# A fused attention, norm and gate layer: the last two steps spread their roots in fp32, half an output product moves ahead, and a search changes place with a tanh

## The chip, the cores and the metric

The kernel runs on one core of one Trainium2 chip. Its time is the device time of one execution in microseconds (us), and the metric is the median over runs. Before the change it is 129.13 us (three runs, 128.83 to 129.57).

## The reference

The input x is [4, 512, 256] in fp32. Cut to what matters, with 16 heads of 16 columns:

```
xn = layernorm(x)
q, k, v = silu(xn @ Wq), silu(xn @ Wk), silu(xn @ Wv)
o  = linear attention with a decay for each head, causal
o  = o * sigmoid((xn @ Wg1) @ Wg2)
og = o * rsqrt(mean(o * o over a head's 16 columns) + 1e-5) * norm_w
s  = og @ Wo
f  = fp8 rounding of (xn * scale), times fp8 rounding of W2, descaled
out = x + s * silu(f)
```

So each output element needs a root for its token and head. A root is computed once for each (token, head) and has to be spread over the 16 columns of the head.

## The kernel before

The work is cut into `STEPS` = 8 steps. A step takes 128 tokens of each of two sequences (`S` = 2, so 256 tokens); steps 0, 2, 4, 6 walk along sequences 0 and 1, steps 1, 3, 5, 7 along sequences 2 and 3. Data lie transposed, channels on the 128 partitions in two halves (`KH` = 2) and tokens along the free side, so that a step's tile of o is 128 x 512. Five engines work side by side, and the order of each engine's instructions is written out by hand: a prologue, a loop over steps 1 to 6, and an epilogue for step 7. Semaphores tie them together; an engine executes its own instructions in order, so a wait holds up all that stands behind it. Step n's scores and outputs overlap with step n+1's projections and with step n-1's norm.

The path of one step through the norm and the output:

- TensorE (PE): `scores(n)`; VectorE (DVE): four `mask(n, r)`, which multiply the scores by the decay mask; PE: `from_state(n)` and `from_chunk(n, half, s)`, which make o; DVE: `gate_o(n)`, which makes og; ScalarE (ACT): `square_o(n)`; PE: `head_sums(n)`, which adds the squares of a head.
- The root: in steps 6 and 7 ACT's `square_root(n)` and DVE's `root_last(n)` (a reciprocal and three small operations on 128 x 64), which leave the root in `rs_full`, in PSUM.
- The spread: `root_pair_last(n)` on DVE splits the root in a rounded part (`rs_hi`, in the fp32r format) and a remainder (`rs_pair`), and multiplies them by `own_block` into `rs_spread` (128 x 256, fp32r). Then PE's `spread_rs(n)` multiplies that with `head_spread`, two matmuls, and adds `rs_in_psum` (`s_rsps`).
- `head_norm(n)` on DVE multiplies og by the spread root into `on`; in step 7 `head_norm_last(s)` does so for each sequence.
- `project_o(n, s)` on PE multiplies `on` by the output weights: in steps 0 to 5 with six fp32r matmuls for each sequence, in steps 6 and 7 with two fp32 matmuls. `product(n)` on DVE multiplies by the silu of f, and `add_x(n)` on POOL (GpSimd) adds x; in step 7 `product_last(s)` and `add_x_last(s)` do both on DVE. SyncE (SP) issues the stores in the order of the steps.

In the epilogue, PE runs `from_chunk(7)`, `spread_rs(6)`, `project_o(5, 1)` (the second half of the output of step 5), `head_sums(7)`, `project_o(6)`, `spread_rs(7)`, three `keep_warm` matmuls on the identity, whose result nobody uses, and `project_o(7)`. DVE runs `root_last(6)`, `root_pair_last(6)`, `gate_o(7)`, `head_norm(6)`, `root_last(7)`, `root_pair_last(7)`, `product(5)`, `head_norm_last`, `product(6)`, and then the last products and sums.

In the prologue, the fp8 rounding of step 1 goes from POOL's `round_y(1)` (it writes `e4_q`) to ACT's `find_over(1)` (values that overflow fp8, into `b_s`), to DVE's `put_nan(1)` (writes `xqT`), to PE's `ffn(1)`. `gate(1)` on ACT is the tanh of step 1's gate. Its result is first wanted by `scores(1)` and `gate_o(1)`. ACT runs `copy_kT(1)`, `gate(1)`, `find_over(1)`, `high_xT(2)`.

`low_xT(2)` and `gate_o(0)` on DVE and `silu_ffn(1)` and `scale_y(2)` on ACT stand behind these in their engines' orders.

Of the kernel before, what the change touches and what calls it, by code (L numbers as in the profile page):

```python
# [5 lines left out]
F32 = mybir.dt.float32  # L6
# [7 lines left out]
P = 128  # L14
# [3 lines left out]
def layer_kernel(nc, x, log_decay, Wq, Wk, Wv, Wo, Wg1, Wg2, norm_w, W2, scale, scale1, out):  # L18
# [27 lines left out]
    with ExitStack() as ctx:  # L46
        def sb(name, shape, dt=F32):
            return ctx.enter_context(nc.sbuf_tensor(name, shape, dt))

        def sem(name):  # L50
            return ctx.enter_context(nc.semaphore(name))
# [19 lines left out]
        root_var = sb("root_var", [P, 2, C])  # L71
        root_sqrt = sb("root_sqrt", [P, 2, C])
        root_inv = sb("root_inv", [P, 2, C])
        wg2_stack = sb("wg2_stack", [P, D], F32R)
        w2_f32 = sb("w2_f32", [P, KH, D])
        w2_y = sb("w2_y", [P, KH, D])
# [110 lines left out]
        ps_u_last = b_x[:, W // 2:W].rearrange("p (k s e) -> p k s e", k=KH, s=S)  # L187
        ps_o_last = b_kv[:].rearrange("p (c z) -> p c z", c=2)[:, :, 0:256]
        ps_out_last2 = b_o[:, 0:512].rearrange("p (s n) -> p s n", s=S)
        ps_rs_last2 = b_o[:, 512:1024].rearrange("p (k t) -> p k t", k=KH)  # L190
        ps_sum_last = b_s[:, 0:C]
        ps_prod_last = [b_kv[:, 0:D], b_kv[:, 512:512 + D]]
# [78 lines left out]
        s_rs = sem("og_rs_steps")  # L271
        s_sqrt = sem("last_square_roots_ready")
        s_lastrs = sem("last_rs_steps")
        s_spread = sem("rs_spread_ready")
        s_rsps = sem("rs_in_psum")
        s_on = sem("on_ready")
# [11 lines left out]
        def need(eng, s, v):  # L288
            if v > 0:
                eng.wait_ge(s, v)  # L290
# [234 lines left out]
        def _(act):  # L525
# [56 lines left out]
            def gate(n):  # L582
                act.wait_ge(s_gateps, n + 1)
                need(act, s_og, n - 1)
                dst = gate_tanh[:, n % 2].rearrange("p c (z t) -> p z c t", z=KH * S)
                src = ps_gate.rearrange("p k (s c t) -> p (k s) c t", s=S, c=2)
                a.activation(dst, src, ACT.Tanh, scale=0.5).then_inc(s_gate, 1)
# [8 lines left out]
            def copy_kT(n):  # L596
                act.wait_ge(s_kTps, n + 1)
                need(act, s_score, n - 1)
                a.activation(kT[:, n % 2], ps_kT, ACT.Copy).then_inc(s_kT, 1)
# [74 lines left out]
            act.wait_ge(s_w2q, 4)  # L674
            a.activation(w2_over[:], w2_q[:], ACT.Copy, scale=E4_OVER).then_inc(s_w2q, 1)
            copy_kT(1)
            gate(1)
            find_over(1)
            high_xT(2)
            act.wait_ge(s_dvec, 4)  # L680
            silu_ffn(1)
# [40 lines left out]
        def _(dve):  # L722
# [137 lines left out]
                v.scalar_tensor_tensor(out=rs_full, in0=rs_err, scalar=-3.0 / ROOT_SCALE, in1=root_inv[:, u],  # L860
                                       op0=ALU.add, op1=ALU.mult).then_inc(s_lastrs, 1)

            def root_pair_last(n):

                k = 4 * (n - (STEPS - 2))
                j = RS_STEPS * (STEPS - 2) + 2 * (n - (STEPS - 2))
                dve.wait_ge(s_lastrs, k + 4)
                v.tensor_copy(rs_hi[:], rs_full).then_inc(s_rs, 1)
                dve.wait_ge(s_rs, j + 1)
                v.scalar_tensor_tensor(out=rs_pair, in0=rs_hi[:].bitcast(F32), scalar=head_parity[:, 1:2], in1=rs_full,  # L870
                                       op0=ALU.mult, op1=ALU.subtract).then_inc(s_rs, 1)
                dve.wait_ge(s_rs, j + 2)
                need(dve, s_rsps, n)
                v.scalar_tensor_tensor(out=rs_spread[:], in0=rs_pair.unsqueeze(1).broadcast_to([P, 4, C]), scalar=-1.0,
                                       in1=own_block[:].unsqueeze(2).broadcast_to([P, 4, C]), op0=ALU.mult, op1=ALU.mult).then_inc(s_spread, 1)

            def head_norm_last(s):
                n = STEPS - 1
                dve.wait_ge(s_rsps, n + 1)
                dve.wait_ge(s_og, n + 1)  # L880
                dve.wait_ge(s_outps, S * (n - 1))
                v.tensor_tensor(on[:, n % 2].rearrange("p k (s c t) -> p s k c t", s=S, c=2)[:, s],
                                og[:, n % 2].rearrange("p c (k s t) -> p s k c t", k=KH, s=S)[:, s],
                                ps_rs.rearrange("p k (s c t) -> p s k c t", s=S, c=2)[:, s], ALU.mult).then_inc(s_onlast, 1)

            def product_last(s):
                n = STEPS - 1
# [111 lines left out]
            gate_o(0)  # L999
            dve.wait_ge(s_pec, 1)  # L1000
            v.tensor_scalar(head_spread[:], ps_spread, -0.75, None, ALU.mult).then_inc(s_dvec, 1)
            exponent(2)
            magic(2)

# [28 lines left out]
            for r in (2, 3, 0, 1):  # L1033
                mask(n, r)
            root_last(n - 1)
            root_pair_last(n - 1)
            gate_o(n)
            head_norm(n - 1)
            root_last(n)
            root_pair_last(n)  # L1040

            product(n - 2)
            for s in range(S):
                head_norm_last(s)
            product(n - 1)
# [5 lines left out]
        def _(pe):  # L1051
# [219 lines left out]
            def spread_rs(n):  # L1271
# [4 lines left out]
                                  start=(half == 0), stop=True, skip_group_check=True)  # L1276
                mm.then_inc(s_rsps, 1)

            def project_o(n, s):
                if n == STEPS - 1:  # L1280
                    pe.wait_ge(s_onlast, s + 1)
                elif s == 0:
                    pe.wait_ge(s_on, n + 1)
                    if known(n + 2):

                        pe.wait_ge(s_mid, mids(n + 1))
                        pe.wait_ge(s_end, ends(n + 1))
                    elif n == STEPS - 2:

                        pe.wait_ge(s_probs, 4 * STEPS)  # L1290
                dst = ps_out[:, s] if n < STEPS - 2 else ps_out_last2[:, s] if n < STEPS - 1 else ps_last[s]
                if n < STEPS - 2:
                    tok = slice(s * P, s * P + P)
                    pe.wait_ge(s_onhi, n + 1)
                    pe.wait_ge(s_woready, 4)
                    for kk in range(KH):
                        t.matmul(dst, on_hi[:, kk, tok], wo_hi[:, kk], start=(kk == 0 and s == 0), stop=False, skip_group_check=True)
                    pe.wait_ge(s_wolo, 1)
                    for kk in range(KH):
                        t.matmul(dst, on_hi[:, kk, tok], wo_lo[:, kk], start=False, stop=False, skip_group_check=True)  # L1300
                    pe.wait_ge(s_onlo, n + 1)
                    for kk in range(KH):
                        mm = t.matmul(dst, on_lo[:, kk, tok], wo_hi[:, kk], start=False, stop=(kk == KH - 1), skip_group_check=True)
                    mm.then_inc(s_outps, 1)
                    return
                for kk in range(KH):
                    mm = t.matmul(dst, on[:, n % 2, kk, s * P:s * P + P], wo_scaled[:, kk], start=(kk == 0 and (s == 0 or n == STEPS - 1)),  # L1307
                                  stop=(kk == KH - 1), skip_group_check=True)
                mm.then_inc(s_outps, 1)
# [89 lines left out]
            scores(n)  # L1399
            head_sums(n - 1)  # L1400
            from_state(n)
            from_chunk(n, 0, 0)
            from_chunk(n, 0, 1)
            from_chunk(n, 1, 0)
            from_chunk(n, 1, 1)
            spread_rs(n - 1)
            project_o(n - 2, 1)
            head_sums(n)
            project_o(n - 1, 0)
            project_o(n - 1, 1)  # L1410
            spread_rs(n)

            keep_warm(3, b_k)
            for s in range(S):
                project_o(n, s)

# [26 lines left out]
```

## Time and profile before

| | |
|---|---|
| median of three runs | 129.13 us (128.83 to 129.57) |
| the profiled execution | 128.68 us |
| its span | 126.9 us |
| PE busy | 114.7 us (90%) |
| DVE busy | 101.7 us (80%) |
| ACT busy | 81.4 us (64%) |
| POOL busy | 80.8 us (64%) |
| mean granted TensorE clock | 0.994 of full speed |

The profiled execution is 1.78 us longer than its span: that part lies around the instructions that the profile records. PE's busy share is an average: matmuls are pipelined and their ends are modelled. In the stretch of the loop it is near 100%, and in the epilogue (from 110.7 us) it falls to six or seven tenths, with DVE at eight or nine.

### The profile page before, as it was taken

To read this page: it belongs to the slowest core of one execution; us is meant where nothing else is said; L and a number is where in the kernel's file an instruction comes from. 1 tells how busy PE (TensorE), PEld (TensorE's weight loads), DVE (VectorE), ACT (ScalarE), POOL (GpSimd) and SP (SyncE) were. 2 spreads that over 40 slices of the span, in tenths; PEclk is the share of its full clock that TensorE was granted. 3 is DMA by queue.
4 is the path that set the end of the run, shared out by engine and by line. 5 is a ranking of instruction groups with operands and counts; after the bars stand their busy time and mean duration, and the time that the engine had idled before them with its cause. 6 is when DMAs were issued, how large, how long until landed. Compare 5 with 4: busy or idle time off the path is not lost.

```text
span 126.9 us, 6394 instructions
## 1 busy us (share of the span) xinstructions
PE 114.7 (90%) x2688; PEld 99.3 (78%) x2688; DVE 101.7 (80%) x271; ACT 81.4 (64%) x156; POOL 80.8 (64%) x119
## 2 busy tenths in 40 slices
PE   3979989988999999999999999999999999867680
PEld 3979889758978898879978898889788987556560
DVE  1899999989895899869994999498939891497781
ACT  7689989969967656684677378558673664811100
POOL 6716599899839683968677884968384839100070
PEclk9999999999999999999999999999999999999997
DMA  2769800020000400033003300150006040000015
GB/s 84 235 175 339 273 3 3 5 45 6 5 0 10 83 0 5 5 62 108 3 5 65 111 0 5 41 132 5 0 20 150 5 126 5 5 5 5 0 67 181
DMA packets 11067, 7.57 MB, mean 60 GB/s; under 512 B 4832, under 2 KB 11040, under 8 KB 11040
## 3 DMA queue, kind: packets, MB, share of 16 engines
q1 hardware_dynamic: 11040, 7.17, 20.2%
q8 instruction: 21, 0.34, 1.1%
q14 instruction: 6, 0.05, 0.1%
HBM read 3.50 MB, written 2.10 MB: 44 GB/s over the span
## 4 chain that ended last, share of the span: by engine, by line
POOL 31%; issue 29%; DVE 20%; ACT 9%; PE 6%; DMA 2%; POOLq 0%; DVEq 0%
POOL e_q L408 5%; POOL e_sum L403 5%; POOL y L441 5%; POOL kd L419 4%; DVE probs L764 4%; POOL rstd L396 3%; POOL own_mid L423 2%; POOL qd L413 2%; DMA x_sb<-in_L_attn_x_dram 2%; POOL on_lo L446 1%; PE b_s L1307 1%; DVE bn L729 1%; POOL own_end L423 1%; DVE og L797 1%; DVE xqT L754 1%
## 5 line engine op out<-in xcount | busy, mean ns | idle before, releaser
L1092 PE MATMUL b_kv<-w_hi,xT_hi 128*128 128x256 f32 x64 | 16.8, 284 | 0.0
L1093 PE MATMUL b_kv<-w_lo,xT_hi 128*128 128x256 f32 x64 | 16.5, 281 | 0.0
L441 POOL TENSOR_TENSOR y<-sg,x_sb 128x512 f32<-128x512 f32 x7 | 9.0, 1286 | 10.4 <-DVE sg L902 10.3
L446 POOL TENSOR_TENSOR on_lo<-on,on_hi 128x512 fp32r<-128x512 f32 x6 | 7.7, 1278 | 12.3 <-ACT on_hi L620 12.3
L403 POOL TENSOR_TENSOR e_sum<-e_y,e_magic 128x512 f32<-128x512 f32 x8 | 10.3, 1285 | 7.2 <-DVE e_magic L748 7.2
L797 DVE SCALAR_TENSOR_TENSOR og<-gate_tanh,b_o 128x512 f32<-128x512 f32 x7 | 4.8, 687 | 11.8 <-PE b_o L1243 11.8
L1095 PE MATMUL b_kv<-w_hi,xT_lo 128*128 128x256 f32 x64 | 12.7, 280 | 0.0
L1243 PE MATMUL b_o<-probs,v_par 64*32 64x64 f32 x896 | 12.6, 222 | 0.0
L413 POOL TENSOR_TENSOR qd<-q_silu,q_decay 128x512 f32<-128x512 f32 x8 | 10.3, 1293 | 3.3 <-ACT q_silu L550 3.3
L1092 PEld LDWEIGHTS b_kv<-w_hi,xT_hi 128*128 128x128 f32 x64 | 12.0, 188 | 0.2 <-issue 0.2
L1093 PEld LDWEIGHTS b_kv<-w_lo,xT_hi 128*128 128x128 f32 x64 | 12.1, 188 | 0.0
L1243 PEld LDWEIGHTS b_o<-probs,v_par 64*32 64x32 f32 x896 | 8.4, 106 | 4.2 <-issue 2.5
L764 DVE TENSOR_TENSOR probs<-b_o,decay_mask 128x512 f32<-128x512 f32 x16 | 10.3, 686 | 1.1 <-PE b_o L1174 1.1
L408 POOL TENSOR_TENSOR e_q<-e_sum,e_magic 128x512 bf16<-128x512 f32 x8 | 10.8, 1345 | 0.5
L550 ACT ACTIVATE q_silu<-b_q 128x512 f32<-128x512 f32 x8 | 4.8, 598 | 9.7 <-PE b_q L1084 9.7
L1174 PE MATMUL b_s<-q_par,kT 32*64 32x128 f32 x256 | 9.3, 276 | 1.0 <-DVE og L797 0.7
L764 DVE TENSOR_TENSOR probs<-b_s,decay_mask 128x512 f32<-128x512 f32 x16 | 10.2, 681 | 0.0
L555 ACT ACTIVATE q_par<-b_q,head_parity 128x512 f32<-128x512 f32 x16 | 10.1, 684 | 0.0
L1095 PEld LDWEIGHTS b_kv<-w_hi,xT_lo 128*128 128x128 f32 x64 | 9.8, 188 | 0.0
L1174 PE MATMUL b_o<-q_par,kT 32*64 32x128 f32 x256 | 9.5, 278 | 0.0
L1174 PEld LDWEIGHTS b_s<-q_par,kT 32*64 32x64 f32 x256 | 7.6, 131 | 2.4 <-issue 2.2
L604 ACT ACTIVATE og_sq<-og 128x512 f32<-128x512 f32 x8 | 5.0, 631 | 6.8 <-DVE og L797 6.8
(205 smaller groups left out, 366.6 us busy)
## 6 DMA issues: line engine op xcount, KB each, us to landing
out_dram<-y SPq DMA_DIRECT2D x7, 256.0 KB, 2.5
x_sb<-in_L_attn_x_dram SPq DMA_DIRECT2D x4, 384.0 KB, 5.4
own_cross<-own_end SPq DMA_DIRECT2D x12, 64.0 KB, 2.0
qd_cross<-qd SPq DMA_DIRECT2D x12, 64.0 KB, 2.4
x_sb<-in_L_attn_x_dram SPq DMA_DIRECT2D x2, 256.0 KB, 3.5
w_f<-in_L_attn_Wq_dram SPq DMA_DIRECT2D x1, 256.0 KB, 3.8
w_f<-in_L_attn_Wk_dram SPq DMA_DIRECT2D x1, 256.0 KB, 4.0
w_f<-in_L_attn_Wv_dram SPq DMA_DIRECT2D x1, 256.0 KB, 4.5
```

What stands on the lines that cost most here:

```text
L403: g.tensor_tensor(e4_sum[:], e4_y[:, n % 2], e4_magic[:, n % 2], ALU.add).then_inc(s_e4sum, 1)
L408: g.tensor_tensor(e4_q[:], e4_sum[:], e4_magic[:, n % 2], ALU.subtract).then_inc(s_e4q, 1)
L413: g.tensor_tensor(qd[:, n % 2].rearrange("p k (s t) -> p k s t", s=S), q_silu[:].rearrange("p k (s t) -> p k s t", s=S), q_decay[:].unsque ...
L441: g.tensor_tensor(y[:, n % 2], sg[:, n % 2].rearrange("p (s d) -> p s d", s=S), x_sb[:, x_tiles(n), :], ALU.add).then_inc(s_y, 1)
L446: g.tensor_tensor(on_lo[:], on[:, n % 2], on_hi[:].bitcast(F32), ALU.subtract).then_inc(s_onlo, 1)
L555: a.activation(q_par[:, n % 2, par], ps_q, ACT.Silu, scale=head_parity[:, par:par + 1]).then_inc(s_qpar, 1)
L764: v.tensor_tensor(probs[:, r], ps_score[r].rearrange("p (s z) -> p s z", s=S), decay_mask[:, r].unsqueeze(1).broadcast_to([P, S, 4 * C]), ...
L1092: t.matmul(dst[:, s], xT_hi[:, u, kk, tok], w_hi[:, w, kk], start=(s == 0 and kk == 0), stop=False, skip_group_check=True)
L1093: t.matmul(dst[:, s], xT_hi[:, u, kk, tok], w_lo[:, w, kk], start=False, stop=False, skip_group_check=True)
L1095: mm = t.matmul(dst[:, s], xT_lo[:, u, kk, tok], w_hi[:, w, kk], start=False, stop=(kk == KH - 1), skip_group_check=True)
L1174: mm = t.matmul(ps_score[r][c * C:c * C + C, cols], kT[rows, u, half, tok], q_par[rows, u, :, half, tok], start=True, stop=True, skip_grou ...
L1243: mm = t.matmul(dst[32 * r:32 * r + 32, c, z:z + C], v_par[rows, u, blk:blk + 2 * E], probs[rows, r, s, i:i + C], start=(half == 0 and s = ...
```

## The change

It has three parts.

1. In steps 6 and 7 the roots are spread in fp32. `root_blocks(n)` replaces `root_pair_last(n)`: one DVE operation multiplies `rs_full` by `own_first` into `rs_blocks` (128 x 256, fp32). `own_first`, 128 x 4, is a new constant, made once in the prologue by one DVE operation. `spread_blocks` replaces `spread_rs`: the same two matmuls, both operands now fp32. In step 7 it is called for each sequence, with half the columns each, into two PSUM areas, and `head_norm_last(s)` waits for its own one. The `keep_warm` calls are two instead of three, and stand ahead of the spread.
2. `project_o(5, 1)` on PE moves from behind `spread_rs(6)` to ahead of `from_chunk(7)`; `product(5)` on DVE moves from behind the roots of step 7 to between `gate_o(7)` and `head_norm(6)`.
3. On ACT, `find_over(1)` comes ahead of `gate(1)`.

```diff
+        own_first = sb("own_first", [P, 4])
+        rs_blocks = sb("rs_blocks", [P, 2, 4, C])
...
+        ps_rs_last = [b_x[:, 0:T], b_o[:, 512:512 + T]]
...
             copy_kT(1)
+            find_over(1)
             gate(1)
-            find_over(1)
             high_xT(2)
...
-            def root_pair_last(n):
-
-                k = 4 * (n - (STEPS - 2))
-                j = RS_STEPS * (STEPS - 2) + 2 * (n - (STEPS - 2))
-                dve.wait_ge(s_lastrs, k + 4)
-                v.tensor_copy(rs_hi[:], rs_full).then_inc(s_rs, 1)
-                dve.wait_ge(s_rs, j + 1)
-                v.scalar_tensor_tensor(out=rs_pair, in0=rs_hi[:].bitcast(F32), scalar=head_parity[:, 1:2], in1=rs_full,
-                                       op0=ALU.mult, op1=ALU.subtract).then_inc(s_rs, 1)
-                dve.wait_ge(s_rs, j + 2)
-                need(dve, s_rsps, n)
-                v.scalar_tensor_tensor(out=rs_spread[:], in0=rs_pair.unsqueeze(1).broadcast_to([P, 4, C]), scalar=-1.0,
-                                       in1=own_block[:].unsqueeze(2).broadcast_to([P, 4, C]), op0=ALU.mult, op1=ALU.mult).then_inc(s_spread, 1)
+            def root_blocks(n):
+
+                u = n % 2
+                dve.wait_ge(s_lastrs, 4 * (n - (STEPS - 2)) + 4)
+                dve.wait_ge(s_ownfirst, 1)
+                v.tensor_tensor(rs_blocks[:, u], rs_full.unsqueeze(1).broadcast_to([P, 4, C]),
+                                own_first[:].unsqueeze(2).broadcast_to([P, 4, C]), ALU.mult).then_inc(s_spread, 1)
 
             def head_norm_last(s):
                 n = STEPS - 1
-                dve.wait_ge(s_rsps, n + 1)
+                dve.wait_ge(s_rsps, n + s + 1)
...
-                                ps_rs.rearrange("p k (s c t) -> p s k c t", s=S, c=2)[:, s], ALU.mult).then_inc(s_onlast, 1)
+                                ps_rs_last[s].rearrange("p (k c t) -> p k c t", k=KH, c=2), ALU.mult).then_inc(s_onlast, 1)
...
             v.tensor_scalar(head_spread[:], ps_spread, -0.75, None, ALU.mult).then_inc(s_dvec, 1)
+            dve.wait_ge(s_hpar, 2)
+            v.tensor_scalar(own_first[:], own_block[:], head_parity[:, 0:1], None, ALU.mult).then_inc(s_ownfirst, 1)
             exponent(2)
             magic(2)
...
             root_last(n - 1)
-            root_pair_last(n - 1)
+            root_blocks(n - 1)
             gate_o(n)
+            product(n - 2)
             head_norm(n - 1)
             root_last(n)
-            root_pair_last(n)
-
-            product(n - 2)
+            root_blocks(n)
             for s in range(S):
                 head_norm_last(s)
             product(n - 1)
...
+            def spread_blocks(n, dst, blocks):
+
+                pe.wait_ge(s_spread, n + 1)
+                for half in range(KH):
+                    mm = t.matmul(dst[:, half], head_spread[:, half].bitcast(F32), rs_blocks[:, n % 2, blocks].rearrange("p j t -> p (j t)"),
                                   start=(half == 0), stop=True, skip_group_check=True)
                 mm.then_inc(s_rsps, 1)
...
             from_state(n)
+
+            project_o(n - 2, 1)
             from_chunk(n, 0, 0)
             from_chunk(n, 0, 1)
             from_chunk(n, 1, 0)
             from_chunk(n, 1, 1)
-            spread_rs(n - 1)
-            project_o(n - 2, 1)
+            spread_blocks(n - 1, ps_rs_last2, slice(0, 4))
             head_sums(n)
             project_o(n - 1, 0)
             project_o(n - 1, 1)
-            spread_rs(n)
-
-            keep_warm(3, b_k)
+
+            keep_warm(2, b_k)
+            for s in range(S):
+                if s == 1:
+                    pe.wait_ge(s_on, n)
+                spread_blocks(n, ps_rs_last[s].rearrange("p (k t) -> p k t", k=KH), slice(2 * s, 2 * s + 2))
             for s in range(S):
                 project_o(n, s)
```

## Rows read from the trace of the kernel before

**Rows 1.** The page's chain that ended last, shares of the span by engine.

```profile
POOL 31%; issue 29%; DVE 20%; ACT 9%; PE 6%; DMA 2%; POOLq 0%; DVEq 0%
```

**Rows 2.** Stretches: start:end, length, busy time per engine, granted clock, DMA share, GB/s.

```profile
33.00:45.00 12.00, 11.91 (x314) 10.06 (x313) 9.91 (x25) 8.23 (x17) 8.92 (x12) 1.00 0.12 25
...
119.30:120.28 0.98, 0.00 (x0) 0.00 (x1) 0.91 (x4) 0.00 (x0) 0.00 (x0) 1.00 0.00 0
```

**Rows 3.** Timeline of ACT, prologue: start, length, engine, line, operation, out<-in, shapes, [idle before].

```profile
24.86 0.59 ACT L587 ACTIVATE gate_tanh<-b_s 128x512 f32<-128x512 f32 x1
25.35 0.59 ACT L562 ACTIVATE b_s<-e_q 128x512 f32<-128x512 bf16 x1
25.87 0.59 ACT L540 ACTIVATE xT_hi<-b_x 128x512 fp32r<-128x512 f32 x1
```

**Rows 4.** Timeline of POOL, prologue.

```profile
23.22 1.73 POOL L408 TENSOR_TENSOR e_q<-e_sum,e_magic 128x512 bf16<-128x512 f32 x1
...
31.30 1.29 POOL L408 TENSOR_TENSOR e_q<-e_sum,e_magic 128x512 bf16<-128x512 f32 x1
```

**Rows 5.** Timeline of DVE, prologue.

```profile
23.01 0.80 DVE L989 SCALAR_TENSOR_TENSOR w_q<-w_f,w_m 128x512 bf16<-128x512 f32 x1
...
24.63 0.87 DVE L995 SCALAR_TENSOR_TENSOR w_fp<-w_over,w_q 128x512 bf16<-128x512 bf16 x1
25.98 0.69 DVE L754 SCALAR_TENSOR_TENSOR xqT<-b_s,e_q 128x512 bf16<-128x512 f32 x1 [0.48 <-ACT b_s L562]
...
30.11 1.29 DVE L764 TENSOR_TENSOR probs<-b_o,decay_mask 128x512 f32<-128x512 f32 x2 [0.25 <-PE b_o L1174]
```

**Rows 6.** Timeline of PE, prologue.

```profile
26.77 0.60 PE L1145 MATMUL b_s<-w_fp,xqT 128*128 128x256 bf16 x4 [0.52 <-issue]
```

**Rows 7.** Timeline of DVE, epilogue.

```profile
114.60 0.22 DVE L868 CAST rs_hi<-b_x 128x64 fp32r<-128x64 f32 x1
...
115.18 0.42 DVE L874 SCALAR_TENSOR_TENSOR rs_spread<-b_x,own_block 128x256 fp32r<-128x256 f32 x1
115.52 0.68 DVE L797 SCALAR_TENSOR_TENSOR og<-gate_tanh,b_kv 128x512 f32<-128x512 f32 x1
116.20 0.69 DVE L845 TENSOR_TENSOR on<-og,b_o 128x512 f32<-128x512 f32 x1
117.76 0.55 DVE L853 RECIPROCAL root_inv<-root_sqrt 128x64 f32<-128x64 f32 x1 [0.87 <-ACT root_sqrt L614]
...
120.14 0.68 DVE L902 TENSOR_TENSOR sg<-b_q,ffn_silu 128x512 f32<-128x512 f32 x1
120.82 0.75 DVE L882 TENSOR_TENSOR on<-og,b_x 128x256 f32<-128x256 f32 x2
121.49 0.68 DVE L902 TENSOR_TENSOR sg<-b_o,ffn_silu 128x512 f32<-128x512 f32 x1
...
123.79 0.42 DVE L896 TENSOR_TENSOR y<-b_kv,x_sb 128x256 f32<-128x256 f32 x1
```

**Rows 8.** Timeline of PE, epilogue.

```profile
113.28 1.68 PE L1243 MATMUL b_kv<-probs,v_par 64*32 64x64 f32 x128 [1.25 <-DVE probs L764]
115.66 0.50 PE L1275 MATMUL b_o<-rs_spread,head_spread 128*128 128x256 f32 x2 [0.70 <-DVE rs_spread L874]
...
120.62 0.83 PE L1313 MATMUL b_kv<-ident 128*128 128x128 f32 x6
121.29 1.99 PE L1307 MATMUL b_s<-wo_scaled,on 128*128 128x256 f32 x8
```

**Rows 9.** Timeline of ACT, epilogue.

```profile
116.23 0.63 ACT L604 ACTIVATE og_sq<-og 128x512 f32<-128x512 f32 x1 [4.23 <-DVE og L797]
```

**Rows 10.** Timeline of POOL and of SP's queue, the last stores.

```profile
120.90 2.61 POOL L441 TENSOR_TENSOR y<-sg,x_sb 128x512 f32<-128x512 f32 x2 [10.32 <-DVE sg L902]
...
123.54 0.37 SPq L361 DMA_DIRECT2D out_dram<-y  x1
...
123.96 0.96 SPq L378 DMA_DIRECT2D out_dram<-y  x2
```

More of the change, by code:

```diff
@@ L273, in layer_kernel @@
         s_lastrs = sem("last_rs_steps")
+        s_ownfirst = sem("own_first_ready")
         s_spread = sem("rs_spread_ready")
@@ L1277, in spread_rs @@
                 mm.then_inc(s_rsps, 1)
+            def spread_blocks(n, dst, blocks):
+                pe.wait_ge(s_spread, n + 1)
+                for half in range(KH):
+                    mm = t.matmul(dst[:, half], head_spread[:, half].bitcast(F32), rs_blocks[:, n % 2, blocks].rearrange("p j t -> p (j t)"),
+                                  start=(half == 0), stop=True, skip_group_check=True)
+                mm.then_inc(s_rsps, 1)
             def project_o(n, s):
```

## The prediction

> **What bounds the kernel now.** I read the page's chain of waits first, then the busy time by stretch, then the timelines of each engine around the two places that the diff touches. The chain names POOL with 31% and "issue" with 29% [rows 1], but in the loop PE is busy 11.91 of 12.00 us, DVE 9.91, POOL 8.92, ACT 8.23 [rows 2]: TensorE has hardly a gap there, and nothing in the diff is in that stretch. Two stretches are left. In the prologue PE sits idle 0.52 us ahead of the fp8 product of step 1 [rows 6], which waits for DVE's xqT; that one waited 0.48 us for ACT's overflow search [rows 5], which ran at 25.35, right behind the tanh [rows 3]. In the epilogue one chain runs through all engines: masks, o, og (115.52), its square (116.23), head sums, root (117.76), spread (120.28), on (120.82), two fp32 output products (121.29 to 123.28), last sum (to 124.21), stores [rows 7 to 10]. PE is idle for 1.25 us ahead of o [rows 8], and for all of 119.30 to 120.28 while DVE finishes the root; the clock stays at 1.00 there, 2.4 GHz [rows 2].
>
> Times below are on the clock of the old trace. The sum is made against the profiled execution's 128.68 us, which is 0.45 under the median of 129.13; the predicted time is put back on the median's level.
>
> **Part 3, the search first.** The search needs POOL's e_q, which ends at 23.22 + 1.73 = 24.95 [rows 4]. ACT is free for it at 24.86, where the tanh now starts [rows 3]. So it starts at about 25.02 in place of 25.35, and xqT at 25.65 in place of 25.98: 0.33 us. Bounds: ACT's slot allows 0.49 and DVE is busy until 24.63 + 0.87 = 25.50 [rows 5], so at most 0.46; POOL's ends are rough, and the search ran at 25.35 without a wait, so at least 0. I take 0.33, by the row's end. The tanh moves from 24.86 to about 25.51, first wanted by the scores of step 1, just ahead of the masks at 30.11 [rows 5]: covered. The copy xT_hi moves from 25.87 to 26.02 and ends at 26.61; its reader on DVE stands behind xqT (ends at 26.34) and four statistics operations: covered, and late by no more than 0.15 if they took no time. PE's product has been waiting 0.52 [rows 6], so it follows by the full 0.33, and behind it ACT's silu, DVE's og of step 0 and the scores of step 1, from which PE runs without a gap. POOL's work up to e_q of step 2 (ends 32.59 [rows 4]) doesn't move, but its reader on ACT, the search of step 2, stands in the loop behind seven operations of that step. I find nothing after that which stays at an absolute time, so the 0.33 reaches the end.
>
> The new constant own_first is one DVE instruction on 4 columns; the nearest row, 64 columns, takes 0.22 [rows 7]. It goes ahead of the exponents of step 2, and DVE has 0.25 of idle time before the masks that follow [rows 5]: cost 0, at most 0.2 if that cover were gone.
>
> **Part 2, the moved half.** project_o(5,1) is six fp32r matmuls of the shape of the spread's two, which take 0.50 [rows 8]: at most 1.5 us, and about 0.9 if they follow one another at 0.12, as the two do. It falls in the 1.25 us in which PE waits for the masks (112.03 to 113.28) [rows 8]; its inputs are those of project_o(5,0), which ran in step 6. Cost 0, at most 0.25 by the upper figure. What it frees: PE has nothing between the spread of step 6 and the head sums.
>
> product(5), 0.68 us with 0.61 from its start to the next one's, leaves the place where it covered PE's last spread (120.14) [rows 7] and stands ahead of head_norm(6). That is weighed below.
>
> **Part 1, step 6.** Removed on DVE: a cast and the pair, 114.60 to 115.18, 0.58 us; the block product is the same 128 x 256 at 0.42 [rows 7]. Blocks: 114.60 to 115.02. og then waits for PE's o, which ends at 113.28 + 1.68 = 114.96 [rows 8]: start 115.05 in place of 115.52, so only 0.47 of the 0.58 is kept. Its square ends at 116.39 (was 116.86 [rows 9]).
>
> The fp32 spread has no row of its own; two fp32 matmuls of the same shape are in L1307: 8 records, two for each matmul, in 1.99 us with the last 0.38 long, so 0.23 a record [rows 8]. Four records: 3 x 0.23 + 0.38 = 1.07 us in place of 0.50, 115.08 to 116.15. Bounds: 0.50 (no dearer than fp32r) and 1.76 (each record double). I take 1.07, since shape and type are the same. The head sums, queued behind it on PE, are due at 116.45: 0.30 of slack. DVE: product(5) from 115.66, head_norm(6) from 116.27 (the spread is there at 116.20), on(6) at 116.96, 0.07 later than now (116.89 [rows 7]). Then project_o(6) from 117.02, and PE is free at 117.02 + 8 x 0.23 = 118.86. Two keep_warm calls are 4 of the old 6 records, 0.11 each [rows 8]: 119.31.
>
> **Step 7.** The root follows og: reciprocal at 117.29 in place of 117.76. Less the 0.58, blocks end at 119.17 in place of 120.22. PE would take them at 119.23, but is free at 119.31. Each sequence's spread is 4 records of 0.11, the last 0.28 long: first ready at 119.31 + 0.33 + 0.28 = 119.92, second at 120.37. on of sequence 0: 119.97 to 120.39 (was 120.82 to 121.24). project_o(7) starts at 120.45 in place of 121.29 and ends at 122.44: 0.84 gained, and the last y ends at 123.37 in place of 124.21 [rows 7].
>
> The end is set by the queue beside it, though. The second on half starts at 120.42, product(6) at 120.76 in place of 121.49 [rows 7]; POOL adds x (its second sum, to 123.51 [rows 10]), SP issues the store of step 6 at 123.54 and the two last ones behind it from 123.96, back to back [rows 10]. The last one left at about 124.45, 0.24 after its data. All of this moves by product(6)'s 0.73, and store 5 is long gone by then. The epilogue gives 0.73.
>
> Sum: 0.33 + 0.73 = 1.06. 128.68 - 1.06 = 127.62 us; at the median's level 128.07.
>
> **Rivals.** (a) The search gives nothing: e_q arrives at 25.3 and not at 24.95. For it: POOL's spans are rough. Against: a row says 24.95, and nothing else holds the search. Gain 0.73: 128.40.
>
> (b) POOL's addition for step 5, which now runs beside the last root, holds up the DVE. product(5) ends at 116.34, so POOL works from 116.40 to 117.68 (half of 2.61 [rows 10]), where today it is idle; the reciprocal is due at 117.29. For it: POOL's e_q took 1.73 beside DVE's w_q, which reads two tensors in SBUF (23.01 to 23.81), and 1.29 at 31.30 [rows 4, 5], so the two engines do hold each other up. Against: the reciprocal reads one tensor, and the operation behind it, which reads two, is due at 117.95. If the reciprocal waited for POOL, it is 0.39 late, the blocks come at 119.56 and PE starts on them at 119.62, not 119.31: 0.31 lost, gain 0.75: 128.38. The Trainium skill ("SBUF", section on the two separate sides) says that VectorE and GpSimd have one pair of ports in common, taken exclusively for a whole instruction by whichever comes first, on VectorE's side only in a two-port mode or with two SBUF inputs; the two e_q rows agree in kind (0.44 longer). By that rule the reciprocal goes free and only a later start of POOL, by 0.27 or more, would cost anything.
>
> (c) Slower: the fp32 spread costs more than the output product's records say, since its weights are fresh each time and it stands in PE's queue ahead of the head sums, of project_o(6) and of the last step. With records twice as far apart, spread 6 ends at 116.84, on(6) at 117.58, PE is free at 119.93, and the second half's spread is ready at 121.75. product(6) starts at 122.14, 0.65 later than now, and with POOL and SP behind it the end as well; less the 0.33 of the search, 0.32 slower: 129.45. It decides from 1.8 times the record's spacing. Against: L1307 changes its weights with every matmul too and shows 0.23.
>
> **How the numbers follow.** Forecast 50%; (a) 22%; (b) 10%; (c) 8%; 10% for more (the search's 0.46, or the second half's spread less late and the last store bound by its data's 0.84: 1.3, 127.83). About 0.5%, 0.65 us, is what a measurement here can tell from no change. Faster by more than that: 0.45 of the forecast's 0.50, half of (a) and of (b) (0.16), since they lie just over the line, and 0.08 of the last: 0.69. Slower: half of (c) and a little, 0.05. Same: 0.26. The range goes from the larger gain with a fast median to half of what lies between (a) and (c): 127.5 to 129.0.
>
> **What would show it.** Right: xqT of step 1 some 0.3 us earlier and PE's gap ahead of it near 0.2; the six matmuls ahead of o without moving o; a spread of 4 records in about 1.07 us in step 6 and 0.6 for a half in step 7; product(6) 0.73 earlier relative to the masks of step 7, and the last stores back to back behind the store of step 6. Wrong: on(6) more than 0.2 late behind a longer spread; a reciprocal that starts when POOL's y ends; masks of step 7 at the old time.

## The result and the profile after

The changed kernel takes 128.55 us (median of 20 runs) where the kernel before took 128.84 in 20 runs beside it. The ratio is 0.9951 with an interval of 0.9929 to 0.9974: 0.63 us faster, between 0.34 and 0.92. The forecast was 1.06 (a ratio of 0.9918), so the direction was right and the size was not: 1.06 lies outside the interval. The ratio is that of the mean times without the slower runs; four of the changed kernel's that it leaves out took only 129.53 to 129.75, and with every run below 140 us counted on both sides it would be 0.9968, some 0.4 us. The profiled execution took 128.26 us with a span of 126.4 (before 128.68 and 126.9), at a granted clock of 1.000.

First the page after: busy time of the engines, the chain that ended last, and the queue of the instruction transfers (number, MB, share).

```profile
PE 116.2 (92%) x2694; PEld 100.5 (79%) x2694; DVE 100.8 (80%) x268; ACT 81.4 (64%) x156; POOL 80.9 (64%) x119
...
POOL 31%; issue 29%; DVE 17%; PE 8%; ACT 8%; DMA 2%; POOLq 0%; DVEq 0%
...
q8 instruction: 21, 0.34, 1.1%
```

DVE's share of the chain fell from 20% to 17% [rows 1] and PE's rose from 6% to 8%. The third line is one that I did not look at before I predicted; it turns out to matter.

The prologue on ACT, the answer to [rows 3]:

```profile
25.06 0.60 ACT L566 ACTIVATE b_s<-e_q 128x512 f32<-128x512 bf16 x1
25.60 0.58 ACT L591 ACTIVATE gate_tanh<-b_s 128x512 f32<-128x512 f32 x1
```

On DVE, the answer to [rows 5] in its first, third and fourth line (the second is the new constant), and then the epilogue, the answer to [rows 7]:

```profile
25.70 0.69 DVE L758 SCALAR_TENSOR_TENSOR xqT<-b_s,e_q 128x512 bf16<-128x512 f32 x1
...
28.70 0.22 DVE L1001 TENSOR_SCALAR own_first<-own_block,head_parity 128x4 f32<-128x4 f32 x1
...
29.83 1.29 DVE L768 TENSOR_TENSOR probs<-b_o,decay_mask 128x512 f32<-128x512 f32 x2
...
110.37 1.29 DVE L768 TENSOR_TENSOR probs<-b_o,decay_mask 128x512 f32<-128x512 f32 x2 [0.86 <-PE b_o L1173]
...
114.22 0.42 DVE L872 TENSOR_TENSOR rs_blocks<-b_x,own_first 128x256 f32<-128x256 f32 x1
...
115.25 0.69 DVE L801 SCALAR_TENSOR_TENSOR og<-gate_tanh,b_kv 128x512 f32<-128x512 f32 x1 [0.61 <-PE b_kv L1242]
115.86 0.69 DVE L900 TENSOR_TENSOR sg<-b_q,ffn_silu 128x512 f32<-128x512 f32 x1
116.46 0.68 DVE L849 TENSOR_TENSOR on<-og,b_o 128x512 f32<-128x512 f32 x1
...
117.50 0.55 DVE L857 RECIPROCAL root_inv<-root_sqrt 128x64 f32<-128x64 f32 x1 [0.37 <-ACT root_sqrt L618]
...
118.96 0.42 DVE L872 TENSOR_TENSOR rs_blocks<-b_x,own_first 128x256 f32<-128x256 f32 x1
...
120.97 0.69 DVE L900 TENSOR_TENSOR sg<-b_o,ffn_silu 128x512 f32<-128x512 f32 x1
...
123.17 0.42 DVE L894 TENSOR_TENSOR y<-b_kv,x_sb 128x256 f32<-128x256 f32 x1
```

PE after, first the product of step 1 in the prologue, the answer to [rows 6], then the epilogue, the answer to [rows 8]:

```profile
26.49 0.60 PE L1144 MATMUL b_s<-w_fp,xqT 128*128 128x256 bf16 x4 [0.16 <-issue]
...
111.58 0.50 PE L1304 MATMUL b_q<-wo_hi,on_hi 128*128 128x256 f32 x2
...
112.90 1.00 PE L1242 MATMUL b_kv<-probs,v_par 64*32 64x64 f32 x77 [0.35 <-DVE probs L768]
114.47 0.74 PE L1242 MATMUL b_kv<-probs,v_par 64*32 64x64 f32 x51 [0.56 <-issue]
115.14 1.13 PE L1282 MATMUL b_o<-rs_blocks,head_spread 128*128 128x256 f32 x4
...
119.02 0.61 PE L1320 MATMUL b_kv<-ident 128*128 128x128 f32 x4
119.47 0.69 PE L1282 MATMUL b_x<-rs_blocks,head_spread 128*128 128x128 f32 x4
119.99 0.61 PE L1282 MATMUL b_o<-rs_blocks,head_spread 128*128 128x128 f32 x4
120.67 1.99 PE L1314 MATMUL b_s<-wo_scaled,on 128*128 128x256 f32 x8
```

Last, the stores on POOL and on SP's queue, the answer to [rows 10]:

```profile
116.62 1.27 POOL L445 TENSOR_TENSOR y<-sg,x_sb 128x512 f32<-128x512 f32 x1 [6.43 <-DVE sg L900]
121.74 1.27 POOL L445 TENSOR_TENSOR y<-sg,x_sb 128x512 f32<-128x512 f32 x1 [3.85 <-DVE sg L900]
```

```profile
123.03 0.37 SPq L365 DMA_DIRECT2D out_dram<-y  x1
123.45 0.96 SPq L382 DMA_DIRECT2D out_dram<-y  x2
```

Reading these against before: the first mask of step 1 is 0.28 earlier (29.83, was 30.11), the first mask of step 7 is 0.38 earlier (110.37, was 110.75), the last y starts another 0.24 earlier (123.17, was 123.79). The last stores are issued 0.51 earlier (123.45, was 123.96), so 0.13 beyond the masks. The forecast had 0.33 for both masks, and beyond them 0.84 for the last y and 0.73 for the stores. The search's part is there in this profile; more than two thirds of the epilogue's gain are missing. And one pair of rows is strange: the 128 equal matmuls of step 7's from_chunk fall into 77 and 51, with 0.56 us between them that "issue" ends, which is to say that no semaphore does. The forecast had them in one piece of 1.68.

In what follows, a **stop** is the time between the starts of two neighbouring weight loads on PE where the next block of instructions is suspected; in from_chunk the loads are normally 0.01 apart. Its place is the number of the second load, counted from PE's first, which is number 0. In after the stop is 0.83 us in front of load 2595.

### The profile page after: what moved, and what is told of

Read it like the earlier page. It is cut to its first block, busy times and chain, and to the rows that moved or that the text cites. A ratio compares the mean times of both kernels' runs of the same rounds, so it can differ in the third digit from the quotient of the medians.

```text
span 126.4 us, 6404 instructions
## 1 busy us (share of the span) xinstructions
PE 116.2 (92%) x2694; PEld 100.5 (79%) x2694; DVE 100.8 (80%) x268; ACT 81.4 (64%) x156; POOL 80.9 (64%) x119
## 4 chain that ended last, share of the span: by engine, by line
POOL 31%; issue 29%; DVE 17%; PE 8%; ACT 8%; DMA 2%; POOLq 0%; DVEq 0%
POOL e_q L412 5%; POOL y L445 5%; POOL e_sum L407 5%; POOL kd L423 4%; DVE probs L768 4%; POOL rstd L400 3%; POOL own_mid L427 2%; POOL qd L417 2%; DMA x_sb<-in_L_attn_x_dram 2%; PE b_s L1314 2%; PE b_o L1314 2%; POOL on_lo L450 2%; PE b_kv L1242 1%; DVE bn L733 1%; POOL own_end L427 1%
## 5 line engine op out<-in xcount | busy, mean ns | idle before, releaser
L1242 PE MATMUL b_o<-probs,v_par 64*32 64x64 f32 x896 | 12.6, 222 | 0.0
```

What stands on the lines that cost most here:

```text
L1242: mm = t.matmul(dst[32 * r:32 * r + 32, c, z:z + C], v_par[rows, u, blk:blk + 2 * E], probs[rows, r, s, i:i + C], start=(half == 0 and s = ...
```

## The experiments

The theory after the first comparison: the stop is PE waiting for the next block of its own instructions. The rival: it belongs to the place, the inputs or the neighbours of that code. A second question was what each part of the change is worth alone. Each kernel was timed in turns with the kernel before on the same chip. Medians of different jobs differ by some tenths, so ratios are compared.

**Search alone, and epilogue alone.** In the first, the kernel before with

```diff
-            gate(1)
             find_over(1)
+            gate(1)
```

and in the second the changed kernel with these two put back.

> Only the third part of the change, on the kernel before: find_over(1) ahead of gate(1) on ACT. It separates the prologue's share. Theory: xqT of step 1 is some 0.3 us earlier, PE passes it on undiminished, and the masks of step 7 start 0.3 us earlier (110.75 before, about 110.4): ratio about 0.9975. Rival: TensorE's stream later gives it back, for example by waiting for its own instructions: ratio 1.000, masks of step 7 at the old time.

> The changed kernel with gate(1) back ahead of find_over(1): parts one and two alone. In the profile of the changed kernel PE stops for 0.56 us in the middle of from_chunk(7), with no semaphore behind it, which leaves the epilogue 0.24 us of gain where 0.73 were forecast. Theory (the stop is a wait for the next block of PE's instruction stream, whose arrival is tied to an absolute cadence): with the masks 0.3 us later the stop is shorter by that, about 0.25 us, and the epilogue alone gains about 0.5 us: ratio 0.996. Rival (the stop is something of the place, such as the moved project_o or the order of the tiles, and keeps its length): gain 0.24, ratio 0.998.

Measured: 0.9983 [0.9950, 1.0017] for the search alone, 0.9940 [0.9907, 0.9973] for the epilogue alone. PE's from_chunk of step 7, first with the search alone, then with the epilogue alone:

```profile
113.65 1.05 PE L1243 MATMUL b_kv<-probs,v_par 64*32 64x64 f32 x83 [1.11 <-DVE probs L764]
115.53 0.69 PE L1243 MATMUL b_kv<-probs,v_par 64*32 64x64 f32 x45 [0.83 <-issue]
```

```profile
113.89 1.85 PE L1242 MATMUL b_kv<-probs,v_par 64*32 64x64 f32 x128 [0.35 <-DVE probs L768]
```

The search alone has the old code at this point and the stop is there too, 1.08 us; the epilogue alone has the new code and a short one of 0.37, inside the 1.85. So the stop does not belong to the new epilogue. Both lengths are off my expectations: I had the masks of step 7 at about 110.4 in the search alone, and they came at 111.11, later than before's 110.75; and in the epilogue alone I had expected some 0.25 of idle time and a ratio of 0.996. An arrival at a fixed time doesn't fit either, since the masks of the two are only 0.24 apart (111.11 and 111.35) and the stops 0.71. From first mask of step 7 to last y the search alone took 13.44 (before 13.04), the epilogue alone 12.34. The time of the search alone settles nothing: 0.33 us is 0.26%, and the interval is 0.34% to either side.

**Moving the instructions.** If the stop sits at an instruction number, more instructions in the prologue shift the code under it. In these four kernels small matmuls, whose results nobody reads, take the place of part of keep_warm, which fills idle time there; only their number differs (20 here for 72 more instructions; 40, 15 and 34 for 152, 52 and 128).

```diff
-            keep_warm(10, ps_score[1])
+            keep_warm(8, ps_score[1])
+            pad_queue(20)
...
+            def pad_queue(count):
+                for i in range(count):
+                    rows = slice(C * (i % 2), C * (i % 2) + C)
+                    r = (i // 2) % 4
+                    t.matmul(ps_score[i % 2][32 * r:32 * r + 32, 0:C], ident[rows, 0:32], ident[rows, 0:C],
+                             start=True, stop=True, skip_group_check=True)
```

> The changed kernel with 72 more PE instructions in the prologue: keep_warm(10) becomes keep_warm(8) and 20 small matmuls on the identity whose result nobody uses (each is four instructions, two weight loads and two matmul passes), in PE's idle time before x arrives. Nothing else moves. Theory (the stop in from_chunk(7) is at a block boundary of PE's instruction stream, counted in instructions): the stop moves from behind weight load 77 of 128 to about weight load 41, and is longer by the 0.4 us that PE gets there earlier, about 0.9 us, if the block arrives at the same time. Rival (it belongs to the place): still behind about load 77, same length.

> As the kernel with 72 more instructions, but 40 small matmuls, 152 more PE instructions in the prologue. Theory (block boundary): the boundary moves 76 weight loads earlier, to about the first of from_chunk(7), where PE waits for the masks anyway, so that most of the stop is hidden and the o of step 7 is ready up to 0.5 us earlier than in the changed kernel: ratio to before about 0.992, if no other dense stretch is hit. Rival (it belongs to the place): stop behind load 77 and the changed kernel's time, ratio 0.995.

> 52 more PE instructions in the prologue (keep_warm(8) and 15 small matmuls in place of keep_warm(10)). Theory (block boundary): the block boundaries at weight loads 2470 and 2595 now fall on the scores of step 7 and on about load 51 of 128 of from_chunk(7); between the two PE has about 4 us instead of 3 in the changed kernel, so there is no stop, or one under 0.3 us, and the last y comes 12.1 to 12.3 us after the first mask of step 7 (12.80 in the changed kernel): ratio 0.991 to 0.993 if the boundaries in the loop cost no more than before. Rival (a stop of the place): 0.995 and a stop behind load 77 of from_chunk(7).

> 128 more PE instructions in the prologue (keep_warm(8) and 34 small matmuls). Theory (block boundary): the boundary at 2595 falls on about load 13 of 128 of from_chunk(7), 4 us behind the one before, no stop there; but the next one, at about 2723, now falls into PE's last 48 weight loads, which come 3 us later: a stop there of up to 1 us, in front of the fp32 spread or what follows. Ratio 0.992 to 1.002. Rival (a stop of the place): 0.995 and a stop behind load 77.

Measured ratios: 72 more 0.9941 [0.9914, 0.9968], 152 more 1.0034 [0.9989, 1.0078], 52 more 0.9999 [0.9964, 1.0033], 128 more 0.9944 [0.9913, 0.9974]. PE with 72 more instructions: the first row of the step-1 scores, then from_chunk of step 7.

```profile
30.57 0.33 PE L1173 MATMUL b_s<-q_par,kT 32*64 32x128 f32 x2 [1.08 <-issue]
...
115.41 1.48 PE L1242 MATMUL b_kv<-probs,v_par 64*32 64x64 f32 x128 [0.62 <-DVE probs L768]
```

The second row is the one to see: 128 matmuls in one piece of 1.48 us, shorter than the 1.68 of before and of the forecast. My expectation of a stop near the 41st load was wrong: there was none. Earlier ones, the first of them in the row above it and another of 0.75 in front of load 1846, had made step 7 late (from_chunk starts 2.51 us after it does in after), and I take it that the block had arrived by then: the queue's transfer for it began at 113.41, 2.00 us ahead of from_chunk, where in after it began at 111.92, 0.98 us ahead. With no stop, the last y starts 12.13 us after the first mask.

With 152 more, from_chunk is in one piece too, but the stop has gone to the next boundary, load 2723, and that load is in the fp32 spread of step 6:

```profile
113.59 1.48 PE L1242 MATMUL b_kv<-probs,v_par 64*32 64x64 f32 x128 [0.35 <-DVE probs L768]
115.37 0.48 PE L1282 MATMUL b_o<-rs_blocks,head_spread 128*128 128x256 f32 x1 [0.30 <-DVE rs_blocks L872]
117.38 0.92 PE L1282 MATMUL b_o<-rs_blocks,head_spread 128*128 128x256 f32 x3 [1.52 <-issue]
```

One record, 1.5 us of nothing, three records, all of the same kind, on inputs that were all there for the first: no theory of inputs makes such a row. After it the clock fell as well (last section), and mask to y became 15.61. That is not every execution: in six of the twelve the mean clock was 0.984 or 0.985 as in this one, and in the others 0.993 to 0.999. With 128 more the same load 2723 is in the head sums, which come in two groups of eight:

```profile
116.90 0.32 PE L1266 MATMUL b_s<-og_sq,head_sum 128*32 128x64 f32 x8
117.68 0.32 PE L1266 MATMUL b_s<-og_sq,head_sum 128*32 128x64 f32 x8 [0.47 <-issue]
```

With 52 more the stop is 0.19 in front of 2595, again inside from_chunk, and mask to y is 12.16, as with 72. Yet its time is that of the kernel before, where I had expected 0.991 to 0.993: its profile has stops of 0.54 in front of 470, ahead of the first masks of step 1, and of 0.92 in front of 1470 (0.48 in before). In this profile, what the epilogue won, stops elsewhere took.

**The unchanged kernel again, and fewer instructions.** In the second, keep_warm(10) gives way to three longer matmuls, 28 instructions fewer.

```diff
-            keep_warm(10, ps_score[1])
+            for _ in range(3):
+                t.matmul(ps_score[1][:, 0:3 * P].rearrange("p (a b) -> p a b", a=3), ident[:],
+                         ident[:].unsqueeze(1).broadcast_to([P, 3, P]), start=True, stop=True)
```

> The changed kernel once more, as the reference for the three layouts beside it and for a second profile. Theory (PE stops where it reaches a block of its instruction stream that has not arrived yet): if there is a stop in from_chunk(7) at all it is again in front of weight load 2595 counted from PE's first, with another length than 0.7 us, since the arrival varies; other stops only at 470, 1470, 1845 or the like. Rival (a stop of the place): the same length at the same load. Ratio to before 0.995.

> 28 fewer PE instructions in the prologue: the ten warm-up matmuls of 128 columns become three of 384 columns. Theory (block boundary): the boundary at 2595 falls on about load 91 of from_chunk(7), so a stop in from_chunk(7) is behind about load 91, up to 0.7 us long; ratio 0.993 to 0.997. Rival (a stop of the place): behind load 77.

Measured: 0.9957 [0.9918, 0.9995] again (the medians of all runs, 129.38 and 129.45, hardly differ), 1.0020 [0.9982, 1.0058] with 28 fewer. PE of the two:

```profile
113.39 1.00 PE L1242 MATMUL b_kv<-probs,v_par 64*32 64x64 f32 x77 [0.36 <-DVE probs L768]
114.69 0.74 PE L1242 MATMUL b_kv<-probs,v_par 64*32 64x64 f32 x51 [0.30 <-issue]
```

```profile
113.94 1.12 PE L1242 MATMUL b_kv<-probs,v_par 64*32 64x64 f32 x91 [0.36 <-DVE probs L768]
115.50 0.63 PE L1242 MATMUL b_kv<-probs,v_par 64*32 64x64 f32 x37 [0.44 <-issue]
```

The cut is at the same 77 as in after. Fourteen loads fewer ahead of it put it at 77 + 14 = 91, to the load. The place is fixed by count. The stop's length is not: 0.57 where after's profile had 0.83. Why 28 fewer are no faster than before isn't settled; its profile has two stops in the loop, 0.88 in front of 1094 and 0.48 in front of 968.

**Parts of the epilogue.** First the fp32 spread with both moves and the search put back; then the kernel before with the two moves only; then the changed kernel with product(5) behind the roots again.

```diff
             gate_o(n)
+            product(n - 2)
             head_norm(n - 1)
...
-            product(n - 2)
...
             from_state(n)
+            project_o(n - 2, 1)
             from_chunk(n, 0, 0)
...
-            project_o(n - 2, 1)
             head_sums(n)
```

This is the second kernel's whole edit; the first is the changed kernel with it (and the search) turned round, the third with its first half alone turned round.

> The kernel before with the fp32 spread alone (root_blocks, spread_blocks by sequence, two keep_warm calls ahead), with project_o(5,1) and product(5) in their old places and the tanh first. It shows what the moves are for. Theory: PE now has the longer spread of step 6 and the six matmuls of project_o(5,1) ahead of the head sums, so that these stay where they were (about 6.2 us after the first mask of step 7) and the 0.58 us saved on DVE in step 6 is lost; only that of step 7 is kept, less the slower spread: last y begins 12.6 to 12.8 us after the first mask (13.04 in the kernel before) if from_chunk(7) has no stop over 0.2 us; ratio 0.997. Rival (the moves add nothing): 12.3, ratio 0.9945 as with parts one and two together.

> The kernel before with the two moves alone: project_o(5,1) ahead of from_chunk(7) and product(5) ahead of head_norm(6), the spread as before. Theory: nothing on the chain of step 7 moves, since the roots of step 6 still hold DVE until 115.5 and o has to wait for that anyway, which also hides a stop of PE of up to 0.5 us: last y 13.0 us after the first mask with a stop in from_chunk(7) under 0.5 us, and about 13.0 plus what the stop has over 0.5; ratio 1.000. Rival (the freed PE time is what brings the gain): 12.7 and ratio 0.997.

> The changed kernel with product(5) back behind the roots of step 7, where DVE waits 0.81 us for the spread in the changed kernel. Theory: on(6) comes 0.15 us earlier, as soon as the fp32 spread of step 6 is there, PE is free before the blocks of step 7 are, and the spread of step 7 starts with them, 0.03 to 0.1 us earlier; a gain too small for the clock: ratio 0.994 to 0.996. Rival: product(5) behind the roots delays head_norm_last or POOL's addition for step 6, and the end is 0.1 to 0.3 us later: 0.997.

Measured: 1.0015 [0.9976, 1.0054] for fp32 alone, 1.0008 [0.9974, 1.0042] for the moves alone, 0.9937 [0.9906, 0.9967] with product(5) back. In fp32 alone, PE has the spread, the half output and the head sums one behind the other:

```profile
116.12 1.13 PE L1282 MATMUL b_o<-rs_blocks,head_spread 128*128 128x256 f32 x4
...
117.88 0.43 PE L1266 MATMUL b_s<-og_sq,head_sum 128*32 128x64 f32 x16
```

The stop of 0.65 before it is of the usual size; from the start of the spread to the head sums 1.76 us pass, where after has 1.52 with the half output gone (115.14 to 116.66). Its mask to last y is 12.88. The square of og ends at 117.58 there, so the head sums at 117.88 are 0.30 behind it; in after it is 0.06 (116.60 and 116.66). That is what the missing room costs in the profile; at a stop of 0.65 the new epilogue has about 12.6. By the ratios neither change alone can be told from nothing, and the two together can (0.9940). The difference between the ratios, some 0.9 us, is more than these 0.3, and the rest isn't explained. The moves' profile can't be read for its whole length, for its clock fell. Stretches of that kernel's trace (columns as in [rows 2]):

```profile
119.30:120.30 1.00, 0.90 (x18) 0.71 (x19) 0.64 (x2) 0.52 (x2) 1.00 (x1) 0.93 0.00 0
120.30:121.30 1.00, 1.00 (x3) 0.79 (x3) 0.83 (x3) 0.00 (x0) 0.21 (x1) 0.50 0.00 0
```

With product(5) back, on(6) starts at 116.88, 5.82 after its first mask, where in after it is 6.09: it waits for nothing but the spread. Of these 0.27, 0.13 are the shorter stop (0.70 for 0.83), so the order gives about 0.14, as expected. The ratio can't be told from after's. No layout tried beats the changed kernel by more than its interval.

## Why the forecast was right in direction and wrong in size

**Part 3, the search.** Right at its place. The search starts at 25.06 (25.02 forecast), xqT at 25.70 (25.65), the tanh is covered. PE's gap ahead of the product of step 1 is 0.16, from 0.52. Rival (a) falls. What failed is the sentence "I find nothing after that which stays at an absolute time". From first mask of step 1 to first mask of step 7 the profiles have 80.54 (after), 80.64 (before), 80.67 (after, again), between 81.00 and 81.73 in nine others, and 82.70 in the moves alone, with stops of 1.11 in front of 1094 and 0.75 in front of 1470: a scatter of more than 1 us around an effect of 0.33, in good part made of stops in front of 1470 (0.48 in before, 0.52 in after, 1.02 in the epilogue alone and 1.03 in fp32 alone). Whether the 0.33 arrives whole at the end is open; it is smaller than the interval of each comparison here.

**Part 2, the moved half.** Right: it ran in PE's wait for the masks, and from_chunk started 0.38 earlier, exactly with the first mask. own_first cost 0.22 in DVE's idle time, and step 1's masks behind it weren't late. What the move does shift is the boundary: six loads more ahead of from_chunk put the cut behind its 77th load and not its 84th (by count that is one load earlier, 2595 and 2596; PE's other instructions presumably fill the rest). The row of before, the stretch from from_chunk's start to the stop's end, shows that the stop was there in front of the 85th (columns as in [rows 2], 84 matmuls in 0.98 us of PE's time):

```profile
113.28:114.27 0.99, 0.98 (x84) 0.91 (x84) 0.85 (x3) 0.00 (x0) 0.00 (x0) 1.00 0.00 0
```

**Part 1.** The spread took 1.13 (1.07 forecast), the halves 0.69 and 0.61 (0.61), the blocks of the root ended at 119.38 and the spread followed at 119.47, 0.09 later (0.14 forecast), so keep_warm cost nothing more than foreseen. Rival (c) falls: it needed records twice as far apart. Rival (b) falls as well: POOL's addition ran from 116.62 to 117.89, over the reciprocal at 117.50, which took its usual 0.55 and started right behind the root. The Trainium skill's rule ("SBUF", section on the two separate sides) had this right. The end was bound by SP as forecast: the store of step 6 at 123.03, the last two from 123.45.

**The step that failed** is the start of og in step 7, "og then waits for PE's o, which ends at 113.28 + 1.68 = 114.96: start 115.05 in place of 115.52, so only 0.47 of the 0.58 is kept". I took 1.68 from one profile as if from_chunk were 128 matmuls; it is 1.48 and a stop, which was 0.19 there and 0.83 in the profile after. In after og starts 4.88 us behind the first mask of step 7, where the forecast had 4.30 and before has 4.77. That is 0.58 of the 0.60 us by which the last y misses its forecast (0.24 for 0.84). In the old epilogue DVE was busy with the cast and the pair until 115.5 while o was ready at 114.96, so about 0.5 more of a stop would have cost nothing. The moves alone, which keep the old spread, show it: their stop is 0.55, and og starts 4.78 behind the first mask, as in before with 0.19:

```profile
117.88 0.68 DVE L797 SCALAR_TENSOR_TENSOR og<-gate_tanh,b_kv 128x512 f32<-128x512 f32 x1
```

The change took that DVE work out, and o now sets the start of og, except for the first 0.15 or so of a stop, which DVE's blocks of the root still cover (with no stop, in 72 more, og follows the blocks directly, 4.19 behind the first mask). What a stop has beyond that passes on whole. Mask to last y against the stop in front of 2595:

| kernel | stop, us | mask to last y, us |
|---|---|---|
| new epilogue, 72 more | none | 12.13 |
| new, 52 more | 0.19 | 12.16 |
| new, epilogue alone | 0.37 | 12.34 |
| new, again | 0.57 | 12.53 |
| new, product(5) back | 0.70 | 12.66 |
| new, 28 fewer | 0.71 | 12.67 |
| new, after | 0.83 | 12.80 |
| old, before | 0.19 | 13.04 |
| old, search alone | 1.08 | 13.44 |

In the new epilogue the rows from 0.19 to 0.83 rise by 0.64 us for 0.64 us of stop. (128 more has no stop there, but one of 0.71 in the head sums, and 12.75.) In the old one, 0.89 us more of stop cost 0.40, and 0.19 + 0.5 = 0.69 for free with 1.08 - 0.69 = 0.39 behind it fits that. The forecast's own sum for the last y, 13.04 - 0.84 = 12.20, comes out where the stop is as in before (12.16 at 0.19), and so does the 0.73 of the last stores: 13.21 behind the first mask in before, 12.44 in 52 more, 0.77 less. So the sum of the engines was right, and a term that changes from run to run was missing. That the total still came within half a microsecond is partly luck: the search's gain is smaller than the scatter of the loop. Over the four profiles with a stop of 0.37 to 0.83 and nothing added to the queue the mean is 12.58: a gain of 0.46 against before's 13.04. The end is set by the last two stores, whose mean in the same four is 12.87 against before's 13.21: 0.34, and with after's 0.28 from the search about 0.6. That is an estimate, for before is one profile, and the old epilogue's other one (the search alone) is 0.40 longer; it fits the 0.63, and the 0.4 that all runs give would ask for less from the search or for longer stops.

**What is shown and what isn't.** Shown: the stop keeps its load number through 28 instructions fewer and 52 more, and goes to the head sums or to the spread when enough are added. The instruction queue moves one block ahead of it. Its row for 111.5 to 112.5 in after, and then the page's line of all transfers from 112.5 to 115.3:

```profile
q8 instruction: 1, 0.02, 6.8%
...
DMA packets 0, 0.00 MB, mean 0 GB/s; under 512 B 0, under 2 KB 0, under 8 KB 0
```

In all twelve profiles with a stop in step 7, that transfer starts 2.2 to 2.9 us ahead of the end of the stop (111.92 and 114.47 in after). Where the stop is in from_chunk, its length goes with how far ahead of from_chunk the transfer starts: with 0.8 to 1.1 us the stop is 0.55 to 1.08, with 1.45 and 1.48 (before and the epilogue alone) it is 0.19 and 0.37, with 1.90 (52 more) it is 0.19, and with 2.00 (72 more) there is none. That the transfer is what releases PE isn't seen in a record, and wasn't tested by itself; what makes it start earlier or later is open.

## To carry to other kernels

A gap on PE in the middle of a run of equal matmuls, ended by "issue", is a term of its own: count the weight loads up to it in two kernels, and look whether the number stays while the code moves. Taking work off one engine's branch of a join hands the join to the other branch, with all the scatter that the first had hidden; so read the other branch's length from more than one execution before you count on the difference. And adding or moving a few matmuls shifts every later boundary, which can cost or give as much (0.2 to 2 us here) as the change that is being measured.

## What the runs showed of the hardware

- PE's instructions arrive in blocks of 16 KB: 21 transfers with 0.34 MB for 5388 weight loads and matmuls, about one for every 256. Where small matmuls run densely PE stops for 0.19 to 2.0 us at fixed load numbers, as if the next block came too late: ten of the thirteen profiles have it at 2595 or 2596 and two at 2723; in the loop it is most often at 1470, and also at 470, 1094 and 1846. The Trainium skill ("Runtime: NRT & Kernel Launch", section on instruction fetch mechanics) gives blocks of 16 KiB or 256 instructions, with which the queue's line agrees, and calls the cost of crossing one mostly hidden, with which these traces don't agree: 0.37 us or more in ten of the thirteen. The forecast, which had no term for it, reckoned as that sentence does.
- With 152 more instructions the granted clock was 0.50, which is 1.2 GHz, from 119.5 to 121.0 and 0.51 from there to 122.6, after a stop of 2.0 us; in the moves alone it was 0.50 from 120.3, after PE had been idle for 0.76 us ahead of the head sums, and the output product of 8 records took 3.47 us there in place of 1.99. In after PE is idle for shorter times in this stretch (0.56 and 0.38) and its mean clock over the run was 1.000. The length of one wait doesn't decide it: in before PE was idle for 0.98 us from 119.30 on, and the clock stayed at 1.00 [rows 2]. A forecast that lets PE wait longer in the epilogue needs that price as a rival.
